# Mamba scan: contraction with C by four tokens, step-times-input rows regrouped in DRAM and kept twice

## What is computed

```python
def _mamba(x, W_in, conv_w, conv_b, W_xp, W_dt, dt_b, A_log, Dp, W_out):
    xz = x @ W_in.T
    xp, z = jnp.split(xz, 2, axis=-1)
    xc = ...                                  # causal conv of 4 taps, then silu
    x_dbl = xc @ W_xp.T
    dt_lo, Bm, Cm = (x_dbl[..., :R], x_dbl[..., R:R + N], x_dbl[..., R + N:])
    dt = jax.nn.softplus(dt_lo @ W_dt.T + dt_b)
    A = -jnp.exp(A_log)

    def step(h, inp):
        xt, dtt, Bt, Ct = inp
        dA = jnp.exp(dtt[:, :, None] * A)
        h = dA * h + (dtt * xt)[:, :, None] * Bt[:, None, :]
        y = jnp.einsum('ben,bn->be', h, Ct)
        return (h, y)
    ...
    y = ys.transpose(1, 0, 2) + xc * Dp
    y = y * _silu(z)
    return y @ W_out.T
x1 = _mamba(xn, ...); xr = jnp.flip(xn, axis=1); x2 = jnp.flip(_mamba(xr, ...), axis=1)
```

## Time and profile before

| | us |
|---|---|
| median of 3 runs | 5022.83 (5010.32 to 5029.96) |
| the profiled execution | 5026.35 |
| its span in the profile | 5024.5 |
| first to last scan, pass 1 | 874.59 |
| first to last scan, pass 2 | 860.70 |

### The profile page before, as it was taken

The page is one execution under the profiler, slowest core; times in us unless marked ns, Lnnn a source line. Parts: engine busy times, 40 slices in busy tenths (PEclk is TensorE's granted clock), DMA queues, the critical chain, the costliest instruction groups (busy, mean ns, idle before and its releaser), DMA issues. The chain is left out here.

```text
span 5024.5 us, 130170 instructions
## 1 busy us (share of the span) xinstructions
PE 3553.1 (71%) x50301; PEld 2406.5 (48%) x50301; DVE 3276.9 (65%) x5840; ACT 2346.7 (47%) x5437; POOL 2511.8 (50%) x2256
## 2 busy tenths in 40 slices
PE   5888888888488688688899744565656545556564
PEld 3666666666366466474477412333333323333333
DVE  5777777776476576562388666566667556666675
ACT  3555555555244344233366554444445444444451
POOL 2555555555343342430133426666667066666772
PEclk8999999999777778788999866777778867777787
DMA  1000000000000000000000028767777187776860
GB/s 49 8 9 9 9 9 9 9 8 8 15 0 6 13 0 6 5 0 24 17 1 0 14 78 184 154 154 165 153 161 163 47 183 159 158 155 156 164 159 31
DMA packets 263394, 333.14 MB, mean 66 GB/s; under 512 B 97056, under 2 KB 127024, under 8 KB 260912
## 3 DMA queue, kind: packets, MB, share of 16 engines
q1 hardware_dynamic: 262832, 325.11, 29.2%
HBM read 306.12 MB, written 18.87 MB: 65 GB/s over the span
## 5 line engine op out<-in xcount | busy, mean ns | idle before, releaser
L3492 ACT ACTIVATE banks<-banks,alog 128x255 f32<-128x255 f32 x2048 | 787.8, 447 | 864.2 <-PE banks L3436 796.8
L3449 PE MATMUL banks<-h,c_spread 128*16 128x32 f32 x32768 | 614.6, 234 | 550.0 <-issue 543.7
L3449 PEld LDWEIGHTS banks<-h,c_spread 128*16 128x16 f32 x32768 | 493.1, 115 | 856.1 <-issue 829.9
L3572 DVE TENSOR_TENSOR_SCAN h<-banks,dBx 128x1024 f32<-128x1024 f32 x256 | 576.0, 2279 | 392.5 <-ACT banks L3492 328.7
L3550 POOL TENSOR_TENSOR dBx<-residual,b_by_state 128x1024 f32<-128x1024 f32 x256 | 601.3, 2362 | 356.4 <-DVE h L3572 293.0
L3572 DVE TENSOR_TENSOR_SCAN h<-banks,norm_featmajor 128x1024 f32<-128x1024 f32 x256 | 576.4, 2277 | 226.2 <-ACT banks L3492 213.8
L3550 POOL TENSOR_TENSOR norm_featmajor<-norm,b_by_state 128x1024 f32<-128x1024 f32 x256 | 601.7, 2361 | 215.5 <-DVE h L3572 161.3
L3436 PE MATMUL banks<-dt_rows,selectors 96*128 96x510 bf16 x1024 | 446.7, 506 | 280.7 <-issue 126.3
L3436 PEld LDWEIGHTS banks<-dt_rows,selectors 96*128 96x128 bf16 x1024 | 87.3, 103 | 392.9 <-issue 212.8
L973 POOL TENSOR_TENSOR weighted<-probs,f 128x1024 f32<-128x1024 f32 x64 | 120.7, 1902 | 215.5 <-DVE f L1024 214.3
L2611 POOL TENSOR_TENSOR out_factors<-out_norms,exponents 128x4 f32<-128x4 f32 x64 | 64.4, 1007 | 288.9 <-DVE out_norms L2776 288.9
(11 more groups left out here) (451 smaller groups left out, 8768.8 us busy)
## 6 DMA issues: line engine op xcount, KB each, us to landing
residual<-mamba_dtx_rows SPq DMA_DIRECT2D x512, 256.0 KB, 5.8
norm<-mamba_dtx_rows SPq DMA_DIRECT2D x512, 256.0 KB, 6.3
dt_rows<-mamba_dt_rows SPq DMA_DIRECT2D x64, 96.0 KB, 7.0
delta_blocks<-A_turned SPq DMA_DIRECT2D x256, 8.0 KB, 1.5
inv_turned<-delta_blocks SPq DMA_DIRECT2D x256, 8.0 KB, 1.7
mamba_dtx_rows<-dtx SPq DMA_DIRECT2D x16, 256.0 KB, 2.3
c_spread<-in_l3a_zero SPq DMA_DIRECT2D x2, 2048.0 KB, 10.5
blocks<-delta_blocks SPq DMA_DIRECT2D x32, 64.0 KB, 2.1
```

Source lines behind the costliest of these rows:

```text
L3449: mm = nc.tensor.matmul(k.bank[OBANK][32 * c:32 * c + TALL, i * SJ:(i + 1) * SJ], spread[:, t, :], h[:, u % 2, :, t], start=s == 0, stop=s ...
L3492: e = fn(per_step(decay[l % 2])[:, 2 * x + j, 1:], k.bank[x][:, j * T + 1:(j + 1) * T], ACT.Exp, scale=mem["A"][:, at:at + 1])
L3572: v.tensor_tensor_scan(flat(h[:, u % 2, 4 * i:4 * i + 4, :]), decay[l % 2], dBx[l % 4], 0.0, ALU.mult, ALU.add).then_inc(q["scanned"], 1)
```

## The change

The contraction takes four tokens at once: the moving operand of a `chunk` matmul is 32 channels by 4 neighbouring tokens (128 columns), the stationary one 32 columns, in which the C of the four tokens stand side by side; of the 4 x 4 products of tokens only those of equal tokens are used later. A step has 8 matmuls where it had 32. `c_spread` shrinks from 256 x 16 to 16 x 144 + 16 columns, a unit's result fills the whole of bank 6 (512 columns, not 256), and `move` and `by_features` pick the used elements out of it: 16 fp32 matmuls of 32 columns where there were 8 of 64. The four channels of a step are neighbours in DRAM, so that what one partition gets is one run of 4 KB; `mamba_dtx_rows` is kept in two copies, and `load_dtx` is four DMAs of 32 partitions, each half of the partitions of a g from its own copy. `dt_rows` is loaded for two units at a time.

```diff
-    d["l3a_zero"] = np.zeros(T * 16, np.float32)
+    d["l3a_zero"] = np.zeros(16 * 144 + 16, np.float32)
...
                 def store_dtx(c):
                     sp.wait_ge(q["dtx_ready"], c + 1)
                     for e in range(SE):
-                        sp.dma_start(mem["dtx_rows"][2 * c:2 * c + 2, e].rearrange("b p t -> p b t"),
-                                     pairs(dtx[:, e, cols(c)])).then_inc(q["dtx_stored"], 16)
+                        for copy in range(2):
+                            sp.dma_start(mem["dtx_rows"][copy, 2 * c:2 * c + 2, e].rearrange("b p t -> p b t"),
+                                         pairs(dtx[:, e, cols(c)])).then_inc(q["dtx_stored"], 16)
...
-        spread = p.sb("c_spread", [P, T, TALL])
+        spread = p.sb("c_spread", [P, NG * 4 * WIDE + 16])
-        rows = p.sb("dt_rows", [SROWS, 2, 2, T], BF16)
-        ysb = p.sb("y_tokens", [P, NI, P])
+        rows = p.sb("dt_rows", [SROWS, 2, 4, T], BF16)
+        ysb = p.sb("y_tokens", [P, NG, P, 4])
...
-                def load_rows(u):
-                    tb, jb = u // SUNITS, u % SUNITS
-                    sp.wait_ge(q["cast"], 2 * NI * u + 2 * NI)
-                    sp.dma_start(rows[:, u % 2], mem["dt_rows"][:, 2 * jb:2 * jb + 2, tb * T:(tb + 1) * T]).then_inc(rows_in[u % 2], 16)
+                def load_rows(v):
+                    tb, kh = v // 2, v % 2
+                    sp.wait_ge(q["cast"], 4 * NI * v)
+                    sp.dma_start(rows[:, kh], mem["dt_rows"][:, 4 * kh:4 * kh + 4, tb * T:(tb + 1) * T]).then_inc(rows_in[kh], 16)
...
                     for g in range(SE):
-                        src = mem["dtx_rows"][tb, g].rearrange("(a r) t -> a r t", r=8)[2 * i:2 * i + 2, 2 * jb:2 * jb + 2, :]
-                        sp.dma_start(kept[n % 4][g * 64:(g + 1) * 64, :].rearrange("p (a x) -> p a x", a=2),
-                                     src.rearrange("a r t -> a (r t)").partition_broadcast(64)).then_inc(dtx_in[n % 4], 16)
+                        for copy in range(2):
+                            lanes = slice(g * 64 + copy * 32, g * 64 + copy * 32 + 32)
+                            sp.dma_start(kept[n % 4][lanes, :], mem["dtx_rows"][copy, tb, g, at:at + 4, :].rearrange("j t -> (j t)")
+                                         .partition_broadcast(32)).then_inc(dtx_in[n % 4], 16)
...
-                    for s in range(8):
+                    part = i // 2
+                    out = k.bank[OBANK][:, part * P:(part + 1) * P].rearrange("p (j w) -> p j w", w=4)
+                    for quad in (2 * (i % 2), 2 * (i % 2) + 1):
                         for c in range(4):
-                            t = i * SJ + c * 8 + s
-                            mm = nc.tensor.matmul(k.bank[OBANK][32 * c:32 * c + TALL, i * SJ:(i + 1) * SJ], spread[:, t, :], h[:, u % 2, :, t],
-                                                  start=s == 0, stop=s == 7)
+                            t, at = part * 64 + c * 16 + quad * 4, (part * 4 + c) * WIDE + quad * TALL
+                            mm = nc.tensor.matmul(out[32 * c:32 * c + TALL], spread[:, at:at + TALL], h[:, u % 2, :, t:t + 4],
+                                                  start=quad == 0, stop=quad == 3)
...
-                    for i in range(NI):
-                        mm = nc.tensor.matmul(k.bank[YBANK][:, i * 64:(i + 1) * 64], ysb[:, i, :], used, start=False, stop=i == NI - 1)
+                    for n in range(NG):
+                        for w in range(4):
+                            mm = nc.tensor.matmul(out[:, n, :, :, :, w], ysb[:, n, :, w], ones[:, :, :, :, w], start=False,
+                                                  stop=n == NG - 1 and w == 3)
...
-                    out = ysb[:].rearrange("p n (a r) -> p n a r", r=8)[:, :, :, 2 * u:2 * u + 2]
-                    fn(out, k.bank[OBANK][:, 0:T].rearrange("p (n a r) -> p n a r", n=NI, r=2),
-                       ACT.Copy).then_inc(q["moved"], 1)
+                    out = ysb[:].rearrange("p n (x i v) w -> p n x i (v w)", x=2, i=NI)[:, :, u % 2, :, 16 * (u // 2):16 * (u // 2) + 16]
+                    fn(out, k.bank[OBANK].rearrange("p (n i v) -> p n i v", n=NG, v=16), ACT.Copy).then_inc(q["moved"], 1)
```

More of the change, by code:

```diff
@@ L3118, in _ @@
                     sp.wait_ge(q["kept"], 48)
-                sp.wait_ge(q["dtx_stored"], 32 * SNC)
+                sp.wait_ge(q["dtx_stored"], 64 * SNC)
                 for n in range(2):
@@ L3368, in mamba_scan @@
     NS = SUNITS * NI
-    TALL = 16
+    NG, TALL, WIDE = 4, 32, 144
     LAG = NI + 1
@@ L3429, in cast @@
                     n, u, i = tb * NS + l, l // NI, l % NI
-                    if i == 0:
-                        pe.wait_ge(rows_in[u % 2], 16 * (tb * (SUNITS // 2) + u // 2 + 1))
+                    kh, row = u // 2, 8 * (u % 2) + i
+                    if u % 2 == 0 and i == 0:
+                        pe.wait_ge(rows_in[kh], 16 * (tb + 1))
                     for x in range(2):
@@ L3434, in cast @@
                         out = k.bank[x].rearrange("p (j t) -> p j t", t=T)[:, :, 1:]
-                        a = 2 * i + x
-                        nc.tensor.matmul(out, mem["sel"][:, 2 * a:2 * a + 2, :].rearrange("r g n -> r (g n)"),
-                                         rows[:, u % 2, :, 1:], start=True, stop=True).then_inc(q["cast"], 1)
+                        nc.tensor.matmul(out, mem["sel"][:, 2 * row:2 * row + 2, :].rearrange("r g n -> r (g n)"),
+                                         rows[:, kh, 2 * x:2 * x + 2, 1:], start=True, stop=True).then_inc(q["cast"], 1)
                 def chunk(tb, l):
@@ L3455, in by_features @@
                     for g in range(SE):
-                        nc.tensor.matmul(by_token(g), mem["diag"][:, g, :], in_eights(xc[:, g, tokens(tb)]), start=g == 0, stop=False)
+                        nc.tensor.matmul(by_token(g), mem["diag"][:, g, :], xc[:, g, tokens(tb)], start=g == 0, stop=False)
                     pe.wait_ge(q["moved"], tb * SUNITS + SUNITS + MOVES)
-                    used = k.ident[:].rearrange("p (c s) -> p c s", s=32)[:, :, 0:TALL]
-                    for i in range(NI):
-                        mm = nc.tensor.matmul(k.bank[YBANK][:, i * 64:(i + 1) * 64], ysb[:, i, :], used, start=False, stop=i == NI - 1)
+                    ones = k.ident[:].rearrange("p (c g a w) -> p g c a w", g=SE, a=4, w=4)
+                    out = k.bank[YBANK].rearrange("p (g n c a w) -> p n g c a w", g=SE, n=NG, a=4, w=4)
+                    for n in range(NG):
+                        for w in range(4):
+                            mm = nc.tensor.matmul(out[:, n, :, :, :, w], ysb[:, n, :, w], ones[:, :, :, :, w], start=False,
+                                                  stop=n == NG - 1 and w == 3)
                     mm.then_inc(q["y_ready"], 1)
@@ L3502, in build @@
                     lanes = slice(64 * g, 64 * g + 64)
-                    dst = spread[lanes, half * n:(half + 1) * n, :].rearrange("p (a s) c -> p a (s c)", s=8)[:, :, 8 * g:8 * g + 7 * 17 + 1:17]
-                    fn(dst, in_eights(mem["C"][lanes, tokens(tb, half * n, n)]), ACT.Copy).then_inc(q["built"], 1)
+                    lo = half * 8 * WIDE + 16 * g
+                    dst = spread[lanes, lo:lo + 8 * WIDE].rearrange("p (x a w) -> p x a w", a=4, w=36)[:, :, :, 0:4]
+                    src = mem["C"][lanes, tokens(tb, half * n, n)].rearrange("p (x a w) -> p x a w", a=4, w=4)
+                    fn(dst, src, ACT.Copy).then_inc(q["built"], 1)
                 def move(tb, u):
```

23 lines of the change are left out of this document (12 added, 11 removed).

## The result

The changed kernel takes 4518.94 us (median of 4 runs, 4515.3 to 4531.89), the kernel before 5021.14 us beside it (5010.32 to 5029.96): a ratio of 0.9005 with a 95% interval of 0.8979 to 0.9031. That is 21 us under the range's lower end of 4540 and 211 us under the forecast of 4730. Nearest is the rival "Loads get cheap" (4550, chance 0.19), by its step time, not by its reason, as the experiments show. Each kernel here was executed four times; in three of the experiments (two runs of 2 KB 3 KB apart, small loads, contiguous `y_tokens`) one execution ran at a mean granted clock of 0.54 to 0.60 and took 5118 to 5568 us, which the ratios and ranges leave out and the medians hold (it moves them by 1 to 5 us). The profiled execution took 4531.89 us (span 4530.0), 494.5 us less than that of before.

A forecast was written before the change was run, and what follows sets the result against it. PE starving for instructions was taken to bound the 3.39 us step; with DMA then setting 2.80 us, 5026.35 - 301.7 - 9 + 15 + 4 - 2 = 4732.7, so 4730 us. The 8-in-10 range was 4540 to 4890.

The forecast's parts named there:

- Loads get cheap: Rival for the loads: longer runs and two copies lift the rate over 220 GB/s, step 2.45 us, 4550 us; chance 0.19.
- PE starves for instructions: Scan steps before the change: PE waits 1.36 us a step for instruction packets, and every other engine waits behind it.
- Chunk at 0.5 us, PE well under the step: Chunk matmuls on PE: 16 records take 0.5 us a step, PE's work 1.3 us, up to 2.6 at the lower clock.
- No instruction gap left: PE in the scans: 126 records last 7 steps, some 19 us, so gaps cost nothing, at most 0.44 us a step.
- SP 2.43 to 2.84 us: Load issues on SP: four a step instead of two, 2.43 us at the least, 2.84 us by the pairs.
- DMA at 193 GB/s, 2.80 us a step: Row loads in the scans: 540 KB a step at nearly the present loads' rate, which sets the step, -301.7 us.
- the first rival: Row loads stay at today's lower 175 GB/s, POOL waits for DMA, 3.09 us a step, 4880 us; DMA or SP chance 0.22.
- by_features inside the loop, +15: Turning matmuls inside the scan loop: doubled records add 2.1 us 14 times, 30 us, half counted, +15 (bounds 0 and 30).
- Tail -4.3 us a pass: Work behind each pass's last scan: 15.2 us today, 10.9 after, -4.3 in each pass, -9 in all.
- Stores +4, fill -2: Second copy's 16 issues on SP cost some 2 us a pass, +4; smaller c_spread fill less two further issues, -2.
- Fewer partitions, less rate: Rival for the loads: 32 partitions give about 90 GB/s, 6.0 us a step, 6370 us; chance 0.08.
- Today's rate stays: Rival for the row loads: DMA full at today's 175 GB/s, 3.09 us a step, 4880 us; DMA or SP chance 0.22.

The follow-up runs named there:

- small loads: Kernel before with each load bringing only 1/32 of the bytes, issues and PE instructions unchanged, result not the layer's: 4499.38 us, ratio 0.8934.
- contiguous `y_tokens`: Changed kernel with one copy and two loads a step to 64 partitions, y_tokens columns contiguous, move in four pieces: 4479.55 us, ratio 0.8908.
- Cut in 2: Changed kernel with each chunk matmul cut in two over the channels, 32 chunk records a step, new loads kept: 4569.0 us, ratio 0.9088.
- The 8 KB test: Changed kernel with one copy, two loads a step to 64 partitions, each partition from two 2 KB runs 8 KB apart: 4788.59 us, ratio 0.9517.
- the fastest version: Changed kernel with one copy, two loads a step, y_tokens contiguous, D term and turning matmuls spread over five steps: 4447.62 us, ratio 0.8866.
- runs2k: Changed kernel with one copy, two loads a step to 64 partitions, each partition from two 2 KB runs 3 KB apart: 4525.73 us, ratio 0.9.
- one64: Changed kernel with one copy, two loads a step to 64 partitions, each partition from one 4 KB run: 4519.54 us, ratio 0.8989.
- the 10 KB kernel: Changed kernel with one copy, two loads a step to 64 partitions, two 2 KB runs 10 KB apart: 4521.84 us, ratio 0.9015.

## Why the prediction was wrong

The two parts of the change, one at a time and together (medians in us, and differences from 5021; 64 records and runs 8 KB apart is the kernel before):

| | runs 8 KB apart | other layout |
|---|---|---|
| 64 records a step | 5021 | 4668 (10 KB apart), 4653 (one run) |
| 16 records a step | 4789 | 4519 to 4526 |

Alone the PE part gives 232 us and the layout 353 to 368; together they give 502, less than the sum. (By the ratios it is 243, 354 to 373 and 500.) Each part alone meets the other's limit: with runs 8 KB apart POOL waits for DMA, with 64 records PE still waits for instructions, and with both changed POOL's product holds. The 4653 is with the new turning of y, which costs more.

- *PE starves for instructions.* Right, and now shown: PE goes on 1.2 to 2.9 us after a packet in each of 64 waits, few bytes in the loads end most of it with 64 records kept, more records bring it back, and packets fell from 418 to 143. The Trainium skill (Runtime: NRT & Kernel Launch, "Instruction fetch mechanics") has instructions come in blocks of 256, and the crossing "mostly hidden". The block size agrees with the earlier trace rows; hidden they are not in this kernel, where 64 of the 84 packets between 3100 and 3600 us cost a wait, 3.2 us in the mean.
- *Chunk at 0.5 us, PE well under the step.* 0.64 us at the higher clock and 1.08 at the lower, inside the bounds; PE at its lower clock takes 2.3 us, forecast up to 2.6.
- *No instruction gap left.* Right, but not for the reason given, that a packet has 19 us to come in. From the third sequence on no packet is needed at all, because the shorter loop body stays with the engine. Cut in 2, where by the same reasoning the cover is 3.7 steps or 9 us, the body is brought again in each round and 23.8 + 7.0 us of 500 are "issue" waits.
- *SP 2.43 to 2.84 us.* Wrong: 1.2 to 1.7 us, 40 to 50% less. The price of 0.607 us belonged to an issue with two runs to 64 partitions; one run to 32 costs 0.302 to 0.421. It decided nothing, since 2.80 was taken from DMA.
- *DMA at 193 GB/s, 2.80 us a step.* **This step failed**: "The source of the new runs is the same DRAM and the sum of bytes the same [...] so I take it much nearer to the rows of the same loads". The 175 to 197 GB/s of the earlier trace rows were not what such bytes cost, but what two runs 8 KB apart cost. The 8 KB test has this very kind of bound (179 GB/s, step 2.97 us, between the forecast and the first rival); without that distance the loads carry 217 GB/s at a share of 0.85, up to 230 in the fastest version, and POOL's products, one every 2.31 us and the pauses, set the step. In the sum, 512 x 2.80 = 1433.6 stood for 1252.99 us: 180.6 of the 200.8 us by which 4732.7 missed 4531.89 (the measured figure holds the pauses of `by_features` as well, for which +15 stood beside it). The prediction weighed the bytes, the length of the runs and the partitions; that the change also removes the distance between two runs, it did not weigh.
- *by_features inside the loop, +15.* Too low. The 14 pauses are 62 us, and 62 to 72 us were recovered. The 32 records were priced at today's 2.12 us for 16, 4.24 us; they take 7.50, as the order of time after the last scan shows:

```profile
3648.55 6.09 PE L3454 MATMUL banks<-h,c_spread 128*32 128x128 f32 x128 [2.42 <-DVE h L3581]
3654.58 1.13 PE L3461 MATMUL banks<-xc,diagonal_d 128*128 128x256 f32 x4
3655.55 7.50 PE L3467 MATMUL banks<-ident,y_tokens 128*128 128x32 f32 x32
```

- *Tail -4.3 us a pass.* 3648.50 to 3663.05 is 14.6 us for 15.2, -0.6: the same dear turning matmuls.
- *Stores +4, fill -2.* Hidden or smaller: the first load is issued at 3005.9 for 3012.3 us and the first scan comes 8.3 us earlier. The 6.4 us lie within the spread of the study, in which the first load comes at 2986 to 3012 us, at 2992 to 3012 in the three kernels with the old contraction.
- *Rivals.* Loads get cheap: its 2.45 us a step is what came (2.447), but its two reasons, longer runs and two copies, give nothing in `runs2k` and `one64`, and its 2.43 us for SP is wrong too. That its number fits is partly luck: any cause that takes the loads below POOL's product ends there. Fewer partitions, less rate: its slowdown is refuted for halves that are in flight together (221 and 218 GB/s). Today's rate stays: it came only where the 8 KB were put back. What the prediction named as the sign of cheap loads, over 215 GB/s and no gaps in POOL, is what the profile shows except for the pauses of `by_features`.

What makes 8 KB slow was not measured. That both runs of each load then fall on the same part of the DRAM is argued. It is also open whether the pair in one load counts or all that is in flight: in both slow kernels the runs of neighbouring steps of a unit, too, start whole multiples of 8 KB from each other. In the 10 KB kernel neighbouring steps still do (40 KB), and only the two runs of a pair do not. The Trainium skill (DMA: Bandwidth & Descriptors, "Latency and other measured facts") tells of a drop where rows stand a large power of two apart, with a pad as the cure; here it shows at 8 KB already, and a pad cures it.

## What to carry to other kernels

A DMA rate read from a trace belongs to the pattern of its addresses: before taking it as a floor for a changed layout, ask which distances the change removes, and try a pad, the cheapest edit of this study (353 us). Where an engine waits for "issue" at equal counts of instructions while the DMA engines are busy, look whether it starves for its own program; here fewer instructions and cheaper loads both helped, and a loop body short enough to stay with the engine ended the waits. Once one engine's instruction is the floor, look for its few regular pauses: two small edits around them gave 62 to 72 us.

## What the hardware showed

- Two DRAM runs of 2 KB read to 64 partitions each: 179 GB/s 8 KB apart, where the loads set the step; 219 at 3 KB and 220 at 10 KB, where POOL does.
- PE's waits for instructions go with the bytes of the loads: those by "issue" before chunks and casts were 206 of 500 us (3100 to 3600) in the kernel before, 61 with loads of 1/32 of the bytes. PE goes on a median of 1.43 us after the packet's end.
- A loop body of 1304 PE records is brought once and then no more; one of 2328 is brought again in each round (11 packets of 16 KB).
- With 128 fp32 columns of the stationary operand 16 bytes apart a matmul record took 0.234 us, contiguous 0.149.
- One issue on SP: 0.573 to 0.607 us for two runs to 64 partitions, 0.444 to 0.592 for one to 64, 0.302 to 0.421 for one to 32 (least to middle).
- The granted clock fell from 0.75 to 0.63 in the scan stretches while PE's busy share rose from 0.59 to 0.88.
